# A state-space stage: products of B for four states on ScalarE and TensorE, seven C products on GpSimd, and a finer order of the work

## The reference

```python
xn = layernorm(h1) * ln_w + ln_b                  # h1 = layernorm(x) * (1 + ca) + sa
x_inner, z = split(xn @ W_in.T)                   # 512 channels each
u = silu(causal_conv(x_inner, 4 taps) + conv_b)
dt_low, B, C = split(u @ W_x.T, [64, 80])         # B and C: 16 states per token
dt = clip(softplus(dt_low @ W_dt.T + b_dt) + 0.001, 0.001, 0.1)
for t in tokens:                                  # for each channel d and state n
    h[d, n] = exp(dt[t, d] * A[d, n]) * h[d, n] + dt[t, d] * u[t, d] * B[t, n]
    y[t, d] = sum_n h[d, n] * C[t, n]
out = ((y + u * D_param) * silu(z)) @ W_out.T + h1    # then x + ga * out
```

## Time and profile before

| what | value |
|---|---|
| median of three runs | 4106.91 us (4103.03 to 4107.72) |
| the profiled execution's span | 4108.2 us |
| state-space stage, from the trace | about 1998 to 3920 us |
| VectorE busy over the span | 3549.2 us, 86% |
| TensorE | 3305.6 us, 80% |
| GpSimd | 2624.4 us, 64% |
| ScalarE | 2321.0 us, 56% |

### The profile page before, as it was taken

One profiled execution on the slowest core, in us unless ns is written; L12 is line 12 of the kernel. 1 busy time (PEld: TensorE's weight loads), 2 busy tenths in 40 slices (PEclk: granted clock), 3 DMA queues, 4 the chain that ended last, 5 costly groups with the idle time before them and its releaser, 6 DMA issues. The chain is left out here.

```text
span 4108.2 us, 61159 instructions
## 1 busy us (share of the span) xinstructions
PE 3305.6 (80%) x21708; PEld 1529.2 (37%) x21708; DVE 3549.2 (86%) x5829; ACT 2321.0 (56%) x4302; POOL 2624.4 (64%) x2459
## 2 busy tenths in 40 slices
PE   5979999999993999999566777777777777776467
PEld 3633333333332555555322232222232232222166
DVE  5768888888854999999359999999999999999967
ACT  5626666666672344444356666666666666666422
POOL 1102323232232888888369999999999999998723
PEclk8969999999996999999888888888888888887689
DMA  4894565655513111110112222212222222222132
GB/s 146 281 188 64 78 84 79 88 80 81 82 33 89 35 44 45 44 48 30 34 44 61 63 65 64 69 47 60 69 65 64 65 69 61 68 57 53 42 95 85
DMA packets 274957, 299.58 MB, mean 73 GB/s; under 512 B 35583, under 2 KB 205686, under 8 KB 274646
## 3 DMA queue, kind: packets, MB, share of 16 engines
q1 hardware_dynamic: 274654, 295.68, 31.4%
HBM read 210.22 MB, written 84.51 MB: 72 GB/s over the span
## 5 line engine op out<-in xcount | busy, mean ns | idle before, releaser
L1727 POOL TENSOR_TENSOR d_dBu<-d_dtu,d_Bn 128x1024 f32<-128x1024 f32 x512 | 1217.5, 2413 | 0.1
L1562 ACT ACTIVATE d_dA<-d_dt,d_decay 128x512 f32<-128x512 f32 x1024 | 690.9, 687 | 404.4 <-DVE d_h L1810 402.1
L752 ACT ACTIVATE b_P<-b_pT 128x512 f32<-128x512 f32 (+1 forms) x1120 | 571.8, 575 | 298.1 <-PE b_pT L658 295.3
L1810 DVE TENSOR_TENSOR_SCAN d_h<-d_dA,d_last_h,d_dBu 128x512 f32<-128x512 f32 x512 | 617.1, 1265 | 14.5 <-ACT d_dA L1562 12.8
L1810 DVE TENSOR_TENSOR_SCAN d_h<-d_dA,d_dBu 128x512 f32<-128x512 f32 x512 | 586.3, 1204 | 40.3 <-ACT d_dA L1562 39.0
L785 DVE CUSTOM_DVE_ANT_0 b_pS<-b_pS,mask_qk 128x512 f32<-128x512 f32 (+1 forms) x768 | 501.7, 690 | 83.6 <-PE b_pS L668 74.3
L630 POOL TENSOR_SCALAR_AFFINE_SELECT b_P<-b_P 128x128 f32<-128x128 f32 (+2 forms) x608 | 192.8, 321 | 515.0 <-ACT b_P L752 503.2
L668 PE MATMUL b_pS<-KS,QS 99*128 99x512 bf16 (+3 forms) x1536 | 475.0, 339 | 28.5 <-PEq L85 21.6
L658 PE MATMUL b_pT<-QS,KS 118*128 118x512 bf16 (+3 forms) x1536 | 449.1, 329 | 3.1 <-ACT b_P L752 2.1
L1817 DVE TENSOR_TENSOR d_h<-d_h,d_C 128x2048 f32<-128x2048 f32 x192 | 434.4, 2262 | 0.7 <-PE d_C L1446 0.7
L1446 PE MATMUL d_C<-d_bc,d_pick 96*128 96x512 bf16 x256 | 114.6, 448 | 396.1 <-DVE d_h L1817 396.1
(11 more groups left out here) (313 smaller groups left out, 5983.2 us busy)
## 6 DMA issues: line engine op xcount, KB each, us to landing
d_Bn<-scratch_bs SPq DMA_DIRECT2D x128, 512.0 KB, 4.9
scratch_parts<-a_part SPq DMA_DIRECT2D x48, 512.0 KB, 4.1
QS<-scratch_parts SPq DMA_DIRECT2D x192, 128.0 KB, 7.4
KS<-scratch_parts SPq DMA_DIRECT2D x192, 128.0 KB, 7.9
scratch_v<-a_v SPq DMA_DIRECT2D x16, 1024.0 KB, 7.7
V<-scratch_v SPq DMA_DIRECT2D x32, 512.0 KB, 11.7
a_x<-in_L_attn_x_dram SPq DMA_DIRECT2D x16, 512.0 KB, 7.7
scratch_o<-b_O SPq DMA_DIRECT2D x16, 512.0 KB, 10.0
```

Of the source, the lines that this page charges most:

```text
L752: act.activation(t[:, heads[0]:heads[-1] + 1, c * CH:c * CH + w], pT[:, place % RING, 0:len(heads) * w].rearrange("p (h w) -> p h w", w=w) ...
L1562: act.activation(dA[:, m % 2, :], dt[:, c.k % 2, m, :], ACT.Exp, scale=decay[:, m, n:n + 1]).then_inc(dA_d, 1)
L1727: pool.tensor_tensor(product(c, n)[:, 2 * j:2 * j + 2, :], dtu[:, c.k % 2, 2 * j:2 * j + 2, :], Bn[:, n // BG % 2, n % BG, :].unsqueeze(1) ...
L1810: dve.tensor_tensor_scan(h[:, n % HS, m, :], dA[:, m % 2, :], product(c, n)[:, m, :], start, ALU.mult, ALU.add).then_inc(scanned, 1)
```

## The change

- **Products of B for states 5, 8, 11 and 14 (PE_B).** GpSimd no longer makes them. Once a chunk, TensorE turns dt * u into [token, channel] layout (turn_step: 16 transposes through the tile y) and the rows of B and C (turn_b: 4 small ones through the bank of C), and ScalarE copies both to SBUF (put_step, put_b). For each of the four states ScalarE makes four products of 512 columns with B as a per-partition scale (stage_product, 7, 5, 4 and 2 decays ahead), and TensorE turns them back (turn_product) with four transposes for each m into the banks dA. The decays of these states go to a new SBUF tile dAs instead, and the scans read decays from SBUF and products from PSUM.
- **C products.** GpSimd has seven (0, 2, 3, 6, 9, 10, 12) and VectorE nine. GpSimd's C rows are spread by DMA from DRAM into three buffers (C is now stored beside B); ScalarE's copy is gone, and TensorE spreads C only for VectorE's states.
- **modulate** goes from VectorE to GpSimd, in front of shift, and scale_bias from turn 8 to turn 6. step_input goes to turn 15.
- **x2e is gone**: x2 of chunk e is loaded into h1 when h1 is free, behind the last B load of the step, and finish adds there.
- **Order.** run() gets tables for c too. ScalarE's other work is placed between single decays (four places a turn instead of two); silu is in turn 7. On TensorE sums of VectorE's and of GpSimd's states stand apart, with turn_product or other work between them.
- Two masks of the attention stage are no longer kept through the later stages.

```diff
-POOL_C = (0, 3, 6, 11)
+PE_B = (5, 8, 11, 14)
+POOL_B = tuple(n for n in range(NS) if n not in PE_B)
+POOL_C = (0, 2, 3, 6, 9, 10, 12)
 DVE_C = tuple(n for n in range(NS) if n not in POOL_C)
...
+HS, BG, BS, CR = 4, 2, 3, 3
+LAG, KEEP, AHEAD = 2, 1, (7, 5, 4, 2)
+NPE, NPB, NPC, NDC = len(PE_B), len(POOL_B), len(POOL_C), len(DVE_C)
+MADE = [2 * sum(i < n for i in POOL_B) for n in range(NS + 1)]
...
+                            for chunk, parts in zip((e, c, q, f), turn):
...
+            def spread_c(at, j):
+                slot = at.times(NPC, j) % CR
+                row = NS + POOL_C[j]
+                wait(sp, hC_pool, at.times(NPC, j + 1 - CR))
+                sp.dma_start(Cn[:, slot, :], S["bs"][row:row + 1, tokens(at)].to_broadcast([P, CH])).then_inc(cn_in[slot], 16)
...
+                    if n == 8 and f is not None:
...
                     wait(sp, b_st, q.times(16, 16))
+                    for j in range(CR - 1):
...
                 if e is not None:
+                    wait(sp, xn2, min(total, e.times(1, 4)))
+                    wait(sp, h1_st, 16 * min(total, e.times(1, 4)))
+                    sp.dma_start(h1[:, :, :], tiles(S["x2"][tokens(e), :])).then_inc(x2_in, 16)
                     wait(sp, x3_d, e.times(1, 1))
...
-                if n == 0:
+                if n in POOL_C:
+                    return
+                if n == DVE_C[0]:
                     wait(pe, lo_d, c.times(1, 1))
                     wait(pe, mid_put, c.times(1, 1))
-                if (n - 1) % NS in POOL_C:
-                    wait(pe, c_ev, c.times(len(POOL_C), POOL_C.index(n - 1) + 1))
-                else:
-                    wait(pe, hC_dve, c.times(len(DVE_C), sum(i < n for i in DVE_C)))
+                    wait(pe, bt_put, c.times(1, 1))
+                wait(pe, hC_dve, c.times(NDC, DVE_C.index(n)))
                 pe.matmul(pC[:, :], pick[:, NS + n:NS + n + 1].to_broadcast([96, P]), bc[:, c.k % 2, :], start=True, stop=True).then_inc(c_mm, 1)
 
...
+                if n in PE_B and c is not None:
+                    turn_product(c, n, (0, 1))
...
+            def own_input(c):
+                wait(pe, silu_u, c.times(1, 1))
+                wait(pe, dtuT_put, c.times(2, 2))
+                wait_before(pe, yz_d, c.times(1, 0), passed)
+                sum_blocks(lambda i, m: diag[i * QB:(i + 1) * QB, m, :], u, True, False).then_inc(y0_mm, 1)
+
+            def turn_b(c):
+
+                wait(pe, act_read, c.times(NF, WX + 1))
+                wait(pe, hC_dve, c.times(NDC))
+                for t in range(CT):
+                    last = pe.transpose(pC[:, t * 2 * NS:(t + 1) * 2 * NS], xb[DR:DR + 2 * NS, t * P:(t + 1) * P], K["ident"][DR:DR + 2 * NS, DR:DR + 2 * NS])
+                last.then_inc(bt_mm, 1)
+
+            def turn_step(c):
+
+                wait(pe, dtu_d, c.times(1, 1))
+                wait_before(pe, yz_d, c.times(1, 0), passed)
+                for t in range(CT):
+                    for m in range(MD):
+                        last = pe.transpose(y[:, t, m * P:(m + 1) * P], dtu[:, c.k % 2, m, t * P:(t + 1) * P], K["ident"][:, :])
+                    if t % 2:
+                        last.then_inc(dtuT_mm, 1)
+
+            def turn_product(c, n, halves):
+
+                i = PE_B.index(n)
+                wait(pe, staged, c.times(CT * NPE, CT * i + CT))
+                for m in halves:
+                    wait(pe, scanned, c.times(NS * MD, MD * n + m - 1))
+                    for t in range(CT):
+                        last = pe.transpose(dA[:, m % 2, t * P:(t + 1) * P], product(c, n)[:, t, m * P:(m + 1) * P], K["ident"][:, :])
+                    last.then_inc(turned_b, 1)
...
+            def sums_dve(c, e, n):
...
-                        sum_state(c, j)
+                        if j in DVE_C:
+                            sum_state(c, j)
+                    if n in PE_B:
+                        turn_product(c, n, (2, 3))
+
+            def sums_pool(c, e, n):
+
+                if c is not None:
+                    for j in SUMS[n]:
+                        if j in POOL_C:
+                            sum_state(c, j)
...
+                ({10: lambda e: output(e, 1)},
+                 {1: turn_b, 2: own_input},
+                 {9: lambda q: project_dt(q, 2), 13: lambda q: (project(q, GT + 1, MD + 1), project(q, GT + 2, MD + 2))},
+                 {}),
+                sums_dve,
                 ({6: lambda e: output(e, 0)},
-                 {2: lambda q: convolve(q, 0), 3: lambda q: convolve(q, 1), 4: lambda q: convolve(q, 2), 5: lambda q: convolve(q, 3),
-                  8: lambda q: project_dt(q, 0), 9: lambda q: project_dt(q, 2), 12: lambda q: project(q, GT, MD), 13: lambda q: project(q, GT + 2, MD + 2)},
-                 {14: lambda f: turn(f, 0), 15: lambda f: project(f, IN, 0)}),
-                sums,
-                ({10: lambda e: output(e, 1)},
-                 {0: lambda q: project(q, IN + 2, 2), 1: lambda q: project(q, IN + 3, 3), 7: project_x, 8: lambda q: project_dt(q, 1), 9: lambda q: project_dt(q, 3),
-                  12: lambda q: project(q, GT + 1, MD + 1), 13: lambda q: project(q, GT + 3, MD + 3)},
-                 {14: lambda f: turn(f, 1), 15: lambda f: project(f, IN + 1, 1)}))
+                 {},
+                 {1: lambda q: convolve(q, 0), 3: lambda q: convolve(q, 1), 4: lambda q: convolve(q, 2), 8: lambda q: project_dt(q, 0), 9: lambda q: project_dt(q, 3), 14: lambda q: project(q, GT + 3, MD + 3)},
+                 {15: lambda f: project(f, IN, 0)}),
+                sums_pool,
+                ({},
+                 {1: turn_step},
+                 {0: lambda q: (project(q, IN + 2, 2), project(q, IN + 3, 3)), 5: lambda q: convolve(q, 3), 7: project_x, 8: lambda q: project_dt(q, 1), 12: lambda q: project(q, GT + 0, MD + 0)},
+                 {14: lambda f: (turn(f, 0), turn(f, 1)), 15: lambda f: project(f, IN + 1, 1)}))
...
+                if n in PE_B and m < 2:
+                    i = PE_B.index(n)
+                    wait(act, scanned, c.times(NS * MD, MD * (PE_B[i - 1] if i else PE_B[-1] - NS) + m + 3))
+                else:
+                    wait(act, scanned, c.times(NS * MD, MD * n + m - 1))
+                to = dAs if n in PE_B else dA
+                act.activation(to[:, m % 2, :], dt[:, c.k % 2, m, :], ACT.Exp, scale=decay[:, m, n:n + 1]).then_inc(dA_d, 1)
+
+            def stage_product(c, n, m):
+
+                for i, of in enumerate(PE_B):
+                    if MD * n + m in [MD * of - back for back in AHEAD]:
+                        t = AHEAD.index(MD * (of - n) - m)
+                        if t == 0:
+                            wait(act, scanned, before(c, of))
+                            wait(act, dtuT_put, c.times(2, 2))
+                            wait(act, bt_put, c.times(1, 1))
+                        act.activation(product(c, of)[:, t, :], dtuT[:, t, :], ACT.Identity, scale=BT[:, t, of:of + 1]).then_inc(staged, 1)
+
+            def put_b(c):
+                wait(act, bt_mm, c.times(1, 1))
+                wait(act, staged, c.times(CT * NPE))
+                act.activation(BT[:, :, :], pC[:, 0:CT * 2 * NS].rearrange("p (t n) -> p t n", n=2 * NS), ACT.Copy).then_inc(bt_put, 1)
+
+            def put_step(c, j):
+                wait(act, dtuT_mm, c.times(2, j + 1))
+                act.activation(dtuT[:, 2 * j:2 * j + 2, :], y[:, 2 * j:2 * j + 2, :], ACT.Copy).then_inc(dtuT_put, 1)
...
-            run(act, first_two,
+            run(act, decays(0),
+                ({},
+                 {},
+                 {3: lambda q: convolved(q, 0), 4: lambda q: convolved(q, 1), 9: lambda q: below(q, 0), 10: lambda q: below(q, 3), 13: lambda q: gate(q, 1), 15: lambda q: gate(q, 3)},
+                 {5: lambda f: normalise(f, 0, (0, 1))}),
+                decays(1),
                 ({0: last_gate},
-                 {0: lambda q: inner(q, 1), 1: lambda q: inner(q, 2), 2: lambda q: inner(q, 3), 8: take_x, 9: lambda q: below(q, 1), 10: lambda q: below(q, 3), 11: step_size,
-                  13: lambda q: gate(q, 1), 14: lambda q: gate(q, 3)},
-                 {4: lambda f: normalise(f, 0, (2, 3)), 11: lambda f: normalise(f, 1, (1,)), 12: lambda f: normalise(f, 1, (3,)), 14: carry, 15: lambda f: turned(f, 1)}),
-                last_two,
+                 {},
+                 {1: lambda q: inner(q, 2), 7: silu, 8: take_x, 9: lambda q: below(q, 1), 10: grow, 11: split_mid, 14: lambda q: gate(q, 2)},
+                 {9: lambda f: normalise(f, 1, (0,)), 13: lambda f: (normalise(f, 1, (1,)), normalise(f, 1, (2,)), normalise(f, 1, (3,))), 15: lambda f: turned(f, 0)}),
+                decays(2),
                 ({},
-                 {2: lambda q: convolved(q, 0), 3: lambda q: convolved(q, 1),
-                  4: lambda q: convolved(q, 2), 5: lambda q: convolved(q, 3), 6: silu, 8: lambda q: (below(q, 0), split_hi(q)), 9: lambda q: below(q, 2),
```

(60 more changed lines are left out.)

125 lines of the change are left out of this document (53 added, 72 removed).

## The result

The changed kernel takes **4078.72 us** (4076.81 to 4087.09, four runs) against 4104.97 us for the kernel before beside it (4102.59 to 4107.72): a ratio of 0.9936, with a 95% interval of 0.9922 to 0.9950. That is 26 us less, where 92 less were forecast; the time lies 3.7 us above the eight-in-ten range, which ended at 4075. The profiled execution took 4077.54 us, its span is 4075.7.

What follows compares the result with a forecast made beforehand. VectorE bounds the state-space stage, GpSimd close behind: 101.0 work plus 4.9 waits, taken as 106.0 us a chunk, saves 96 over 16 chunks; 4107 - 96 + 2 = 4013 us, own range 3990 to 4032, eight in ten 3960 to 4075.

Steps and rivals of the forecast that it cites:

- the waits: VectorE's waits in the state-space stage, 4.9 us a chunk in all; less than 3 or more than 8 would show it wrong.
- state 4: VectorE waits 1.3 us a chunk for state 0's sum, which TensorE makes only after state 1's sum and a convolution.
- state 7: VectorE waits 1.3 us a chunk because GpSimd's scale_bias waits for the statistics and so delays product 7.
- state 11: VectorE waits 1.0 us a chunk for its first decay, behind ScalarE's other work in turn 10.
- the rest: Odd chunks, semaphore latencies and the output product's wait: 1.3 us a chunk, half of the kernel before's 2.8.
- rival D: Slower: TensorE's stretches fall to 1.2 GHz, adding 11.2 us a chunk, for 4192 us; chance 0.10.
- VectorE's work: In the state-space stage, three C products and modulate less bring it from 109.2 to 101.0 us a chunk.
- GpSimd's work: In the state-space stage, fewer B products, more C products and modulate bring it from 104.2 to 100.5 us a chunk.
- Start and end: Of the state-space stage: modulate once in the open and two C loads ahead of the first B load, +2 us.
- finish waits for x2: GpSimd's finish waits about 2 us a chunk for x2's load, issued only after product 15.
- C: Rival: GpSimd becomes the bound at 108.3 us a chunk through its waits, for 4050 us; chance 0.25.
- B: Rival: waits hide in each other, VectorE runs at its work plus 1.3, 102.3 us a chunk, 3954 us; chance 0.17.

Runs made afterwards that it cites:

- fill9: The changed kernel with twelve filling transposes ahead of the first matmul for C and twelve more ahead of state 8's in turn 9; 4109.58 us.
- sb8: The changed kernel with scale_bias back at turn 8 instead of turn 6; 4063.62 us.
- sum8: The changed kernel with state 8's sum moved from turn 10 to turn 11, behind state 11's first turned products; 4059.81 us.
- x2early: The changed kernel with the load of x2 into h1 issued ahead of the last load of B rows; 4070.11 us.
- best6: The changed kernel with the five edits and the earlier load of x2, the last split step left on VectorE in bf16 at turn 13; 4011.49 us.
- conv1: The changed kernel with only one tap of four computed in each convolution; 4054.42 us.
- the five edits: Changed kernel: scale_bias at turn 8, twelve filling transposes, state 0's sum at turn 2, state 8's at turn 11, third convolution split by taps; 4037.59 us.

## Why the prediction was wrong

It failed at one term of the sum: the waits, "4.9" a chunk, measured 8.6. That is 3.7 of the 3.8 us a chunk by which 106.0 missed 109.8; the prediction had itself named more than 8 as a sign of being wrong. The amounts of work held. Over all 16 chunks VectorE waits 138.0 us (without the wait ahead of the first scan of all); by the terms of the sum, in us a chunk:

| term | forecast | measured |
|---|---|---|
| state 4 | 1.3 | 2.2 |
| state 7 | 1.3 | 1.5 |
| state 11 | 1.0 | 1.0, for another engine |
| the rest | 1.3 | 3.9 |

- **The rest, +1.3**, is the step that failed. It was put at half of the 2.8 waited before, with no place worked out, and measured 3.9: 2.6 of the missing 3.7. It is spread: state 9 0.7 (ScalarE's decays, behind dt's projections), the second gating 0.6, the statistics 0.5, state 0 0.5, state 10 0.4, state 15 0.4, the others together 0.8. States 9 and 10 and the gating stand behind TensorE's stretch of turns 9 and 10, which ran at the low level in every chunk; the odd chunks of fill9 show what state 10 and the gating owe to that. For the statistics modulate on GpSimd was not counted. Of states 0 and 15 no run here shows the cause.
- **State 4, +1.3**: the mechanism was right and the size off, 2.2 a chunk. 1.4 is what the order costs at the high level; seven chunks of fifteen paid 2.95 to 4.30. The low level was put wholly into rival D, as if a kernel had it or not. It comes stretch by stretch: a part of it belonged into the forecast's own sum.
- **State 7, +1.3**: right in mechanism and size, 1.4 before the first scan and 0.1 before the third. But as a price it was wrong: taken away by itself it came back in good part at ScalarE and at state 0 (sb8).
- **State 11, +1.0 by ScalarE**: the number is luck. It waits 1.0, for TensorE's order (sum8 took it away).
- **VectorE's work**, 101.0: measured 101.2. **GpSimd's work**, 100.5: 99.9. Its waits were put at 4.5; they are 9.9, since it waits for a VectorE that is itself late.
- **TensorE**, 92: busy 91.8. **ScalarE**, 85: 83.5. A staging, 0.79: 0.708. The scans of the turned states as long as the others: yes. Start and end, +2: the start is 2.2 later.
- **finish waits for x2, 2 us**: 2.6, mostly off the path, as x2early showed.

Rival D's mechanism is thus half true and its sign not; by the granted clock the fuller TensorE did lose low stretches (0.91, from 0.86). C was not the case; B was far off. The forecast of 4013 was within reach of the change's own work: with the order mended and one gap filled the same division of work runs at 4011 (best6), with the 4.9 us of waits a chunk that the forecast had. That 4013 came out as 4079 is the order of TensorE's and GpSimd's small pieces and the level of TensorE's clock under them, not their amount. What single removals give does not add up, and how the 66 us divide between order and level stays open.

## What to carry to other kernels

When the bounding engine is relieved until others are nearly as full, most of the saved work can come back as waits: here 5.8 us a chunk of the 8.0 saved. So a remainder of waits may not be scaled down from the kernel before; go through every place where the engine waits for another. Price each wait at both levels of TensorE's clock, and count as price the pieces of work that stand ahead of the awaited one in its engine's queue, down to a single sum of 1.1 us. A wait removed can come back at the next place whose cover it was, often on another engine, and two edits can save the same thing: judge an order by a joint edit, not by the sum of single ones. And look at every edit's trace for what it changed elsewhere; several of the gains here lay in another place than the edit.

## What the hardware did that was not expected

- A VectorE instruction with both operands in SBUF does not run beside GpSimd's, whatever its type: 0.68 us of work took 2.6 us in every second chunk, 9.47 once (conv1), through two boundaries between GpSimd instructions, and 16.59 once (x2early), through five. GpSimd loses as well: the pair of products beside it took 5.11 us, not 4.68. The Trainium skill (SBUF — State Buffer, SBUF: two separate sides) has the first part, an exclusive lock for the whole instruction; that the waiting one can be passed over at a boundary it does not say.
- With twelve transposes in a gap the granted clock was up behind it in 11 of 14 chunks; the same twelve in another gap ran at 1.2 GHz themselves, in every chunk but the first, and the high level was back behind them in the odd chunks alone.
- These kernels spread more from run to run (4027 to 4049 us for the five edits) than the kernel before (4102 to 4113 in seventeen runs). Why was not tried. Two things that the traces show vary by chance and are large enough: the split step's rare holds (7 to 14 us each) and the number of low stretches ahead of state 4 (some 2 us each). That they make the spread is a guess.
